# Products of parts in two stages of a decoder: linear attention's projections and two of three output sources of the coattention, with the copies and subtractions that they need

## The reference

```python
q = (x @ Wq.T); k = (x @ Wk.T); v = (x @ Wv.T)      # 16 heads of 16; x is the normalised input
q, k = _rope(q, k)
q = elu(q) + 1; k = elu(k) + 1
K_sum = K_sum + k_t; KV = KV + k_t[..., :, None] * v_t[..., None, :]     # over the tokens, in order
Y_t = (q_t @ KV) / max(q_t @ K_sum, 1e-6)
return Y @ Wo.T
```

```python
s = (c @ w_c + b_c)[:, :, None] + (q @ w_q + b_q)[:, None, :] + einsum('bcd,bqd,d->bcq', c, q, w_cq) + b_cq
a = softmax(s, axis=2)
c2q_att = einsum('bcq,bqd->bcd', a, q)
b_att = softmax(max(s, axis=2), axis=1)
q2c_att = einsum('bc,bcd->bd', b_att, c)[:, None, :]
z = concatenate([c, c2q_att, c * c2q_att, c * q2c_att]) @ W_l.T + b_l
```

## Time and profile before

| what | value |
|---|---|
| median of 3 runs | 2564.86 us (2560.75 to 2569.78) |
| profiled execution, its own time | 2563.12 us |
| its span, first to last instruction | 2561.2 us |
| PE busy / DVE / ACT / POOL over the span | 84% / 61% / 48% / 41% |
| mean granted TensorE clock | 0.921 of full speed |
| linear attention, first to last PE work | 1178.1 to 1524.3 us |
| coattention, first to last PE work | 1532.5 to 1721.2 us |

### The profile page before, as it was taken

How to read it: one execution, slowest core, us unless ns; L and a number is a source line. 1 busy time by engine, 2 the same in 40 slices (tenths; PEclk the granted TensorE clock), 3 DMA queues, 4 the chain that set the end, 5 groups by cost and what they waited for, 6 DMA issues and landing times. The chain is left out here.

```text
span 2561.2 us, 45780 instructions
## 1 busy us (share of the span) xinstructions
PE 2154.4 (84%) x16918; PEld 1522.0 (59%) x16918; DVE 1573.9 (61%) x3193; ACT 1221.2 (48%) x1956; POOL 1052.0 (41%) x1204
## 2 busy tenths in 40 slices
PE   7699999986676379975999979984499999999996
PEld 5465666654555258863666658872276767666674
DVE  5477777775887746543777754557555555454552
ACT  2366666643111155543555543324446565564742
POOL 3987777720000033206555412210355555454533
PEclk8799999997878689997999998996699999999998
DMA  5000000000000233301111000003245444444422
GB/s 212 1 2 1 0 0 0 0 1 8 5 5 2 66 140 124 137 27 42 28 27 26 10 6 16 15 8 129 103 102 103 100 98 102 95 88 109 84 66 33
DMA packets 62562, 135.95 MB, mean 53 GB/s; under 512 B 10688, under 2 KB 46736, under 8 KB 55568
## 3 DMA queue, kind: packets, MB, share of 16 engines
q0 software_dynamic: 30976, 52.45, 10.1%
q1 hardware_dynamic: 31504, 82.41, 9.2%
HBM read 100.22 MB, written 34.60 MB: 53 GB/s over the span
## 5 line engine op out<-in xcount | busy, mean ns | idle before, releaser
L3036 ACT ACTIVATE f_h<-bank,f_b 128x512 f32<-128x512 f32 x256 | 175.9, 687 | 280.1 <-PE bank L176 272.8
L176 PE MATMUL ring<-f_w2hi,f_hidhi 128*128 128x256 f16 x1024 | 279.2, 273 | 6.1 <-DVE f_hidlo L3073 3.8
L3073 DVE TENSOR_TENSOR f_hidlo<-f_h,f_hidhi 128x512 f16<-128x512 f32 x256 | 177.3, 693 | 172.6 <-ACT f_hidhi L3037 172.6
L176 PE MATMUL ring<-f_w2hi,f_hidlo 128*128 128x256 f16 x1024 | 279.1, 273 | 0.0
L176 PE MATMUL ring<-f_w2lo,f_hidhi 128*128 128x256 f16 x1024 | 279.1, 273 | 0.0
L3127 POOL DMA_INDIRECT out<-f_y,f_to_row x128 | 211.9, 1656 | 47.6 <-issue 34.1
L176 PE MATMUL bank<-f_xthi,f_w1hi 128*128 128x512 f16 x512 | 194.9, 381 | 4.9 <-DVE f_w1lo L3056 4.9
L176 PE MATMUL bank<-f_xtlo,f_w1hi 128*128 128x512 f16 x512 | 194.8, 380 | 0.0
L176 PE MATMUL bank<-f_xthi,f_w1lo 128*128 128x512 f16 x512 | 194.8, 380 | 0.0
L1869 POOL COPY c_from_row<-c_token 128x5 uint32 (+1 forms) x8 | 1.5, 184 | 424.3 <-POOLq L1592 345.7
L3037 ACT ACTIVATE f_hidhi<-bank,f_b 128x512 f16<-128x512 f32 x256 | 173.9, 679 | 0.0
(11 more groups left out here) (537 smaller groups left out, 5899.1 us busy)
## 6 DMA issues: line engine op xcount, KB each, us to landing
f_raw<-in_e_w SPq DMA_DIRECT2D x32, 1024.0 KB
c_raw<-in_e_w SPq DMA_DIRECT2D x16, 1024.0 KB, 5.8
slots_out<-c_y POOLq DMA_DIRECT2D x8, 640.0 KB, 3.7
x<-in_x SPq DMA_DIRECT2D x1, 4096.0 KB
tokens<-c_xn SPq DMA_DIRECT2D x16, 256.0 KB, 2.4
tokens<-f_xn SPq DMA_DIRECT2D x16, 256.0 KB, 2.4
out<-x SPq DMA_DIRECT2D x1, 4096.0 KB, 14.3
wb<-in_wb SPq DMA_DIRECT2D x1, 3096.0 KB, 31.8
```

Source lines behind the costliest of these rows:

```text
L176: mm = pe.matmul(out, left[a], right[b], start=first and n == 0, stop=last and n == 2)
L3036: act.activation(h32[n % 4][:, :], src, ACT.Gelu_apprx_tanh, bias=bias).then_inc(sig["h_full"], 1)
L3073: dve.tensor_tensor(hid_v[1][:, it, at], h32[n % 4][:, :], hid_v[0][:, it, at], ALU.subtract).then_inc(sig["h_lo"], 1)
```

## The change

Linear attention: the weights `c_qkv` and `c_out` (2048 columns) are split before the stage's loop and written back in place as two float16 halves: ACT makes the high copy into a borrowed buffer (`by_cos`), DVE subtracts into another (`by_sin`) and copies that into the weights' place, ACT copies the high half there. In each turn ACT's copies `copy_x` and `copy_o` now write float16, DVE makes the low parts (`low_x`, `low_o`, new) from the same PSUM bank, and the three projections and the output are products of parts. `project_qk` is cut into `project_high` (both products that use the high part of x) and `project_low`, and the order of calls in `half` changes on PE, ACT and DVE.

Coattention: the weights of sources 0 and 1 are split before the loop (ACT, DVE; 1024 columns). In each turn ACT makes two more copies per sequence (the high parts of c2q and of cc), DVE subtracts the low part of c2q (`low_c2q`), POOL that of cc. The products k = 0 and 1 are products of parts, k = 2 stays float32. POOL's addition of the bias row waits for `similar` of this pair, which is later than `xn_ready`. DVE copies both sequences' q2c first and signals `q2c_read` from the copy itself, then makes both low parts, then both `w_eff`.

```diff
@@ linear_attention @@
-        w_qkv, w_o = (tiles(mem.w(n), KT) for n in ("c_qkv", "c_out"))
+        w_in, w_cols = mem.wb[:, WB_AT["c_qkv"][0]:WB_AT["c_out"][1]], KT * 4 * D
+        w_parts = [w_in.bitcast(F16)[:, k * w_cols:(k + 1) * w_cols] for k in range(2)]
...
-                def project_qk(u, i, t):
-                    if t == 0:
-                        pe.wait_ge(u["xn_t_ready"], i.now)
-                        pe.wait_ge(u["on_ready"], i.before)
+                def project_high(u, i, t):
+                    pe.wait_ge(u["xn_high_ready"], i.now)
+                    pe.wait_ge(u["on_ready"], i.before)
                     for h in range(KT):
-                        mm = pe.matmul(u.ring_bank[t], u.xt_v[:, h, t * P:(t + 1) * P], w_qkv[:, h, 0:QK],
-                                       start=h == 0, stop=h == KT - 1)
+                        for k in range(2):
+                            pe.matmul(u.ring_bank[t], u.xt_v[0][:, h, t * P:(t + 1) * P], w_qkv[k][:, h, 0:QK],
+                                      start=h == 0 and k == 0, stop=False)
+                def project_low(u, i, t):
+                    pe.wait_ge(u["xn_low_ready"], i.now)
+                    for h in range(KT):
+                        mm = pe.matmul(u.ring_bank[t], u.xt_v[1][:, h, t * P:(t + 1) * P], w_qkv[0][:, h, 0:QK],
+                                       start=False, stop=h == KT - 1)
...
                 def output(u, i):
-                    pe.wait_ge(u["on_t_copied"], i.now)
+                    pe.wait_ge(u["on_high_ready"], i.now)
+                    pe.wait_ge(u["on_low_ready"], i.now)
...
+                dve.wait_ge(sig["w_high_made"], 1)
+                dve.tensor_tensor(w_half[1], w_in, w_half[0], ALU.subtract).then_inc(sig["w_low_made"], 1)
+                dve.wait_ge(sig["w_low_made"], 1)
+                dve.tensor_copy(w_parts[1], w_half[1]).then_inc(sig["w_low_placed"], 1)
...
+                def low_x(u, i):
+                    dve.wait_ge(u["xn_high_ready"], i.now)
+                    dve.tensor_tensor(u.xn_t[1][:, :], u.low, u.xn_t[0][:, :], ALU.subtract
+                                      ).then_inc(u["xn_low_ready"], 1)
+                def low_o(u, i):
+                    dve.wait_ge(u["on_high_ready"], i.now)
+                    dve.tensor_tensor(u.on_t[1][:, :], u.low, u.on_t[0][:, :], ALU.subtract
+                                      ).then_inc(u["on_low_ready"], 1)
...
@@ coattention @@
-                        pe.wait_ge(u["c2q_ready"], i.now)
+                        pe.wait_ge(u["cq_low_ready"], i.now)
...
-                        pe.wait_ge(u["cc_ready"], i.now)
+                        pe.wait_ge(u["cc_low_ready"], i.now)
...
+                        if k < 2:
+                            split_product(pe, out, [a[:, h, tok] for a in u.mid_v[q][k]],
+                                          [w[:, k, h, :] for w in w_split], k == 0 and h == 0, False)
+                        else:
+                            mm = pe.matmul(out, u.xt_v[q][:, h, tok], u.we_v[q][:, h, :], start=False,
+                                           stop=h == KT - 1)
...
                 pe.wait_ge(sig["w_q_ready"], 1)
+                pe.wait_ge(sig["w_low_made"], 1)
                 last = in_parities(pe, pair)
...
+                        act.activation(u.cq_parts[q][0][:, :], u.c2q_out, ACT.Copy).then_inc(u["cq_high_ready"], 1)
+                    for u in twins:
+                        act.wait_ge(u["cc_ready"], i.now)
+                        act.activation(u.cc_parts[q][0][:, :], u.cc_t[q][:, :], ACT.Copy).then_inc(u["cc_high_ready"], 1)
+
+                act.activation(w_parts[0][:, :], w_mid, ACT.Copy).then_inc(sig["w_high_made"], 1)
                 norm(0, Turn(0, None), 0)
...
-                        pool.wait_ge(u["xn_ready"], i.now)
+                        pool.wait_ge(u["similar"], i.now)
...
+                        pool.wait_ge(u["cc_high_ready"], i.now)
+                        pool.tensor_tensor(u.cc_parts[q][1][:, :], u.cc_t[q][:, :], u.cc_parts[q][0][:, :], ALU.subtract
...
-                        order.step(dve.tensor_copy(u.q2c[:, :], u.q2c_out))
-                        order.wait()
-                        dve.sem_inc(u["q2c_read"], 1)
+                        dve.tensor_copy(u.q2c[:, :], u.q2c_out).then_inc(u["q2c_read"], 1)
+                    for u in twins:
+                        low_c2q(u, q, i)
+                    for u in twins:
+                        dve.wait_ge(u["q2c_read"], i.now)
```

More of the change, by code:

```diff
@@ L2065, in front @@
                     for t in range(NT):
-                        project_qk(w, j, t)
+                        project_high(w, j, t)
+                        project_low(w, j, t)
                     project_v(w, j)
@@ L2105, in half @@
                         turn_keys(w, j, 1)
+                        turn_queries(w, j, 1)
                         turn_keys(w, j, 0)
@@ L2392, in front @@
                         shift(u, j)
+                    low_x(w, j)
                     for t in range(NT):
@@ L2427, in half @@
                         take_first_keys(w, j)
+                    low_o(u, i)
+                    if w:
                         for t in (1, 0):
@@ L2458, in coattention @@
                                                       for n in ("xn", "xn_t", "c2q_t", "cc_t", "w_eff"))
+            u.cq_parts, u.cc_parts = ([[ctx.enter_context(nc.sbuf_tensor(f"e_{n}_{part}{p}{q}", [P, W2], F16))
+                                        for part in ("hi", "lo")] for q in range(2)] for n in ("cq", "cc"))
             u.c_v, u.sw_v = (tiles(t[:, :], KT) for t in (u.c_t, u.sim_w))
-            u.xt_v, u.cq_v, u.cc_v, u.we_v = ([tiles(t[:, :], KT) for t in both]
-                                              for both in (u.xn_t, u.c2q_t, u.cc_t, u.w_eff))
+            u.xt_v, u.we_v = ([tiles(t[:, :], KT) for t in both] for both in (u.xn_t, u.w_eff))
+            u.mid_v = [[[tiles(t[:, :], KT) for t in parts[q]] for parts in (u.cq_parts, u.cc_parts)] for q in range(2)]
             u.a_v = tiles(u.a[:, :])
@@ L2495, in product @@
                     for h in range(KT):
-                        left = (u.cq_v[q], u.cc_v[q], u.xt_v[q])[k][:, h, tok]
-                        right = (w_l[:, 1, h, :], w_l[:, 2, h, :], u.we_v[q][:, h, :])[k]
-                        mm = pe.matmul(u.out[:, t * D:(t + 1) * D], left, right, start=k == 0 and h == 0,
-                                       stop=k == 2 and h == KT - 1)
+                        out = u.out[:, t * D:(t + 1) * D]
+                        if k < 2:
[4 more added lines that the diff above has]
+                                           stop=h == KT - 1)
                     if t == 1 and k == 2:
```

89 lines of the change are left out of this document (58 added, 31 removed).

## The result

| | before | after |
|---|---|---|
| median of the runs | 2566.41 us (2560.75 to 2569.78) | 2520.26 us (2518.09 to 2522.30) |
| span of the profiled execution | 2561.2 us | 2520.6 us |
| a turn of linear attention | 20.89 us | 18.92 us |
| a turn of the coattention, once warm | 21.7 to 21.9 us | 19.9 to 20.0 us |

The ratio is 0.9822, 95% interval 0.9801 to 0.9843: faster by 1.8%, 46 us by the medians, 40.6 by the profiled spans.

What follows compares the result with a forecast made beforehand. PE was taken to bound both stages. Linear attention's 29 us and the coattention's 11 make 40 off the profiled 2563.12, 2523.1; with the median 1.7 above that execution, forecast 2524 us, own range 2517 to 2533, whole range 2509 to 2541.

Steps and rivals of the forecast that it cites:

- PE sets both stages; 2.09 us a turn saved in linear attention: PE bounds both stages; float16 products of parts take 1.05 + 0.52 + 0.52 us a turn off it.
- The loads are hidden: PE's float16 products: each 0.098 us load of the stationary operand is hidden within the 0.109 us step.
- Rival 3: Every float16 product on PE: loads come out in the open, 49 us more, 2614 us; chance 0.02.
- DVE at 17.0 us a turn: Linear attention: two low-part subtractions add 1.37 us to DVE's 15.6, in a turn of some 18.9.
- Rival 1: DVE becomes the bound in linear attention, leaving 1.0 us a turn of PE's saving: 2538 us; chance 0.15.
- `low_o` costs 0.2, the `d_kv` stall shrinks, waits stay near 1 us: PE's waits in a turn of linear attention, laid out engine by engine, giving net 1.8 us a turn.
- Times 16: 29 us: Linear attention: net 1.8 us a turn over 16 turns, 29 us less; ends 12 and 48.
- The weights' split costs nothing, 2.3 at most: Before linear attention's loop: under 9 us of splitting fits 14.20 us of idle DVE; 2.3 if DVE's copy delays POOL's gathers.
- The coattention: 1.7 us a pair: Per coattention pair: 1.05 us from products of parts plus 0.66 us from the second sequence's earlier q2c copy.
- Net 11 us there: Coattention: seven turns give 11.9 us, the last pair's products 1.7, the start costs 2.7; ends 2.5 and 15.
- Rival 2: Coattention: `low_c2q` waits for POOL's subtractions through the shared port, the gain is gone, 2537 us; chance 0.07.
- Rival 4: PE's stalls in linear attention go too: 2.6 us a turn, 53 us in all, 2512 us; chance 0.11.

Runs made afterwards that it cites:

- order_only: The kernel before with linear attention's new order on PE, ACT and DVE, products still float32, no subtractions: 2561.67 us, ratio 0.9990, turn 20.73 us.
- half_low: The changed kernel without two of the four low-part-of-x products in linear attention's query/key projection: 2523.80 us, ratio 0.9844 to the kernel before, turn 18.62 us.
- parts_old_order: The kernel before with linear attention's products of parts in the old order, coattention as before: 2550.95 us, ratio 0.9953, turn 20.12 us.
- q2c_only: The kernel before with only the q2c copies of both sequences issued first and signalling by themselves: 2557.33 us, ratio 0.9983.
- start_late: The changed kernel; in coattention ACT normalises the first pair before the weights' high copy, and DVE instead of PE awaits their low parts: 2520.12 us, ratio 0.9829.
- co_only: The kernel before with only the coattention changed, linear attention as before: 2546.65 us, ratio 0.9935.
- bias_early: The changed kernel with POOL adding the bias row as soon as the pair is normalised, as before the change: 2526.83 us, ratio 0.9865 to the kernel before.

## Why the prediction was right, and where it was not

The forecast was 2524 us (its own sum gives 2524.8), the measured medians 2520.26 and, the second time, 2523.87. Of 40 us by the sum, 40.6 came in the profiled spans. That this is so close is in part luck: linear attention gave 1.8 us less than I had, the coattention 4.9 more, of which 3.0 were a clock that I had not counted on, and the rest of the program took 2.5 back.

- **PE sets both stages; 2.09 us a turn saved in linear attention.** Right. Between `order_only` and the changed kernel, which share the order, the turn falls by 1.81 us; `half_low` shows that most of what leaves PE leaves the turn. That is shown for linear attention; for the coattention no run took PE's work away by itself, and there the reading rests on PE's 19.16 busy of 20.00 us.
- **The loads are hidden.** Right: 0.109 us a step with a load of 0.098 in each. The page "TensorE: Matmul & The Clock Gate" of the Trainium skill (Part 3, The mechanism) would have them in the open; the runs contradict it for these shapes. Rival 3 is out.
- **DVE at 17.0 us a turn.** Wrong, the mis-sized term: 15.45. I added 1.37 us and did not see that the moved steps give 1.39 back, in `d_shift`, which no longer meets POOL's addition, and in `q_stack`. That the net of 1.8 us came out at 1.97 fits this, but no run separates it. Rival 1 would have been nearer without the new order: `parts_old_order` has 16.58 us of DVE and gains 0.77 a turn, where rival 1 had 1.0.
- **`low_o` costs 0.2, the `d_kv` stall shrinks, waits stay near 1 us.** 0.17; gone as a wait; 0.85 in all. Right, though the two larger waits, 0.43 and 0.25, are others than I named.
- **Times 16: 29 us.** 27.2. The steady turns gave what was asked, but the last turn became 1.8 us longer (15.34 to 17.11), and `order_only` with 17.26, both at a clock of 1.00, shows that this is the new order, which has nothing to interleave there.
- **The weights' split costs nothing, 2.3 at most.** The upper case came in part: POOL's gather was held up and the first statistics came 1.57 us later. Not by DVE's copy, as I had put it, but by its subtraction.
- **The coattention: 1.7 us a pair.** Measured 1.9 in the warm turns. Of it `q2c_only` shows 0.7 to 0.8 by itself in three turns, where I had 0.66; that leaves some 1.2 for the products and the moved bias row, where I had 1.05.
- **The start of the coattention: 2.7 us.** 2.96, by the copy and the wait named, as `start_late` shows.
- **Net 11 us there.** The mis-sized term of the coattention: 15.9 in the profile, past my upper end of 15. Seven turns with products and the tail gave 14.9 (my terms: 11.9 + 1.7), the start took 3.0, and the first turn, which carries no products and which I had not counted, gave 4.0. Of these, 3.0 are the higher clock in that turn: with it low, the same turn takes 21.8. `co_only`, which had the low clock, gives 12.3.
- **Rival 2.** Not in this kernel, since the bias row moved: 1.28 us for the two low parts, as forecast. `bias_early` shows the collision and that it costs 0.3 us a turn and 1.7 at the start, not the whole gain. POOL still holds up DVE elsewhere: the two scalings of `e_sim_w` take 1.8 us beside POOL's subtractions, as they took 1.9 before beside its additions, and 0.55 without.
- **Rival 4.** The waits for `d_kv` and for the mask did go, but 0.43, 0.25 and 0.17 us came in their place, so the turn saved 1.97 us and not 2.6.

## What to carry to other kernels

A cheaper product and the order that feeds it are one change: here the order alone gave 0.16 us a turn, the products alone 0.77, and both 1.97. Before judging the engine that gets the extra work full, look for instructions on it that take far longer than the shortest of their kind, and for what GpSimd does beside them; a moved step can give that time back. Where an experiment is to show an effect of a few us, compare the turns of the loop, not the whole time, since the clock around a stage's boundary moves as much.

## What was not expected of the hardware

- A VectorE instruction on two columns (`d_shift`) took 1117 ns on average in one order, where it ended each time with a GpSimd addition of 1.27 us, and 315 in another, where it did not meet it.
- Two subtractions of two SBUF inputs on VectorE took 1.28 us by themselves and 2.97 beside GpSimd's additions; an indirect DMA's issue on GpSimd took 2.57 instead of 0.95 us beside one VectorE subtraction of 2.29.
- TensorE's granted clock over a turn with the same instructions came out at either level depending on the kernel, 18.8 against 21.8 us, and 4.1 us of transposes just ahead of it did not raise it.
